# One core, a layer pair over 16 sequences: a new written order for every engine, and two waits on GpSimd

## The chip, the cores and the metric

The kernel runs on one core of a Trainium2 chip. The metric is the device time of one execution, in microseconds (us); lower is better. The core has five engines with instruction streams of their own: PE (TensorE, matmuls), DVE (VectorE), ACT (ScalarE), POOL (GpSimd) and SP (SyncE, which here only issues DMAs). They meet through semaphores.

## The reference, cut to what matters

The input is x of 16 sequences, 512 tokens, 128 channels. Two layers, each an attention part and a feed-forward part, each with a residual and a layer norm:

```python
x = layernorm(x + L0_attn(x))   # RWKV time mixing and channel mixing
x = layernorm(x + L0_ffn(x))    # soft binary tree: 255 gates, 256 leaves
x = layernorm(x + L1_attn(x))   # rms norm, 16 heads of 8 channels, RoPE, causal softmax
x = layernorm(x + L1_ffn(x))    # 16 experts, the 2 best by softmax, 2 shared ones
```

The time mixing has a key k, a value v and a receptance r of 512 channels, two scans over the tokens, a quotient, and a product with sigmoid(r). The tree multiplies gate probabilities down 8 levels. The experts take the two largest of 16 probabilities per token.

## The kernel before, in words

A sequence is a batch b of 512 tokens, kept as 128 partitions x 4 token tiles or as 128 channels x 512 tokens. All 16 batches go through one software pipeline. ORDER (from line 50) is a list for each engine, written out by hand. An entry `lag:step` means that in turn t the engine does this step for batch t − lag; run() (L276) walks the list turn by turn, 20 turns in all. So in one turn five different batches are in work: time and channel mixing at lags 0 to 2, the tree and RoPE at lag 2, the attention at lags 2 and 3, the experts at lags 3 and 4. An engine does its steps strictly in that order; each step first waits for what it needs (`until`, `reached`) and then raises a semaphore (`raised`). The line in the profile is that of the instruction, or of the helper that issues it (L488 is every plain copy of ACT, L905 every matmul, L638 every scalar_tensor_tensor).

The steps that matter here:

- `row0` to `row39` on PE compute the scores whose maxima `rowmax0` to `rowmax39` on DVE take (L725, L728), through two banks in turn. `max_parts` (L731) then splits the maxima into three bfloat16 parts in four dependent operations on DVE (L733, L638, L737, L739). `maxT` on PE (turn_maxima, L1068) transposes them, `maxT_out` on ACT copies them and `max_rows` on SP sends them by DMA to the queries. Only then `score0` to `score39` and `exp0` to `exp39` begin. I call the first the row stage, the second the score stage.
- The experts: `gb0` to `gb15` on PE spread a gate over all partitions in bank G. The even ones are multiplied with the input by DVE (`u0`, `u2`, ... L808). The odd ones are copied by ACT (`spread1`, ...), then multiplied on POOL (`u1`, `u3`, ... gated_input, L436). `expert0` to `expert15` on PE use them.
- Time mixing, four chunks c of 128 channels: `k`, `v`, `r` on PE; `clamp`, `kv`, `ksum`, `kvsum`, `wkv`, `inverse` on DVE (L651, L657, L662, L667, L638, L675); `k_exp`, `k_first`, `r_tanh` on ACT; `r_sig`, `wk`, `gated`, `rwkv` on POOL (L385, L381, L390, L395). `r` of chunk c waits for `clamp` c (L924).
- Channel mixing: `cmk` on PE, `cmk_tanh` on ACT, `silu` on DVE, `cmr_sig` and `cmr_sum` on POOL (L403, L408), `y0` on DVE (L694), which waits for cmr_sum.
- `tree0` to `tree7` on DVE (L638): two dependent operations per level, twice as many values at each.
- `largest0`, `others`, `largest1`, `gates` on DVE (L784 to L802): the two picks of the router, small operations on 128x64. `others` writes `left` (L638). After `others` the semaphore `pick` stands at 5 for the batch.
- `moments` n on DVE and `root` n on POOL (L344 to L355) prepare a layer norm; `norm` n on ACT applies it. `res` on POOL (L399) adds the residual; `x1_gain`, `x1_bias` on POOL (L372, L376).

Three forms of working on SBUF matter: an operation of DVE may read PSUM and one SBUF operand (rowmax, kv, u, clamp) or two SBUF operands (max_rest, left, tree, the scans); POOL reads SBUF alone.

## Time and profile before

| | |
|---|---|
| median of 3 runs | 1956.96 us (1956.66 to 1959.65) |
| the profiled execution | 1953.77 us, span 1951.9 us |
| busy in the span | PE 1677.3 us (86%), DVE 1554.8 (80%), ACT 1009.0 (52%), POOL 889.5 (46%) |
| mean granted TensorE clock | 0.962 of full speed |
| one turn in the middle of the run | 109.9 us |

The page of the profile gives the busy time of each engine, the chain of work that ended last, and groups of instructions. The timeline view gives start and duration in us, engine, line, operation, output <- inputs and a count; what stands in brackets at the end is how long the engine sat idle before it and what ended that. Several like instructions in a row are merged into one line, so ends of neighbouring rows may overlap a little. In the profile `prob`, `tree` and `x` are also names for buffers that hold other values at other times: u writes `prob`, and the thing called x in `thr<-thr,x` is x0.

### The profile page before, as it was taken

The page shows a single profiled execution, that of the slowest core. Times are in us where ns is not written, and L with a number is a line of the kernel's source. Part 1 is how long each engine was busy: PE and PEld are TensorE (multiplying, and loading weights), DVE is VectorE, ACT ScalarE, POOL GpSimd, SP SyncE. Part 2 cuts the span into 40 slices and gives each one's busy share as a digit, 9 for nine tenths or more (in the row PEclk, how much of TensorE's full clock was granted, in tenths as well). Part 3 has the DMA queues.
Part 4 walks back from the last instruction along what each step waited for, and adds up shares of the span by engine and source line. Part 5 has one row for each costly group of instructions (what it writes and reads, how often), then busy time and mean ns, then how long its engine had stood idle before and what let it go on. Part 6 is the DMA issues. An engine that isn't in the chain of part 4 may idle for free.

```text
span 1951.9 us, 34254 instructions
## 1 busy us (share of the span) xinstructions
PE 1677.3 (86%) x12161; PEld 1088.7 (56%) x12269; DVE 1554.8 (80%) x3386; ACT 1009.0 (52%) x1998; POOL 889.5 (46%) x1120
## 2 busy tenths in 40 slices
...
GB/s 98 0 6 54 2 53 5 45 16 18 45 3 60 2 55 7 38 24 14 49 2 60 2 55 8 33 29 10 53 2 61 2 55 1 31 26 22 35 7 6
DMA packets 66924, 53.39 MB, mean 27 GB/s; under 512 B 8322, under 2 KB 65474, under 8 KB 66754
## 3 DMA queue, kind: packets, MB, share of 16 engines
...
q10 hardware_dynamic: 3552, 1.65, 0.3%
...
## 4 chain that ended last, share of the span: by engine, by line
PE 49%; DVE 33%; POOL 6%; ACT 5%; issue 5%; SPq 1%; DMA 0%; ACTq 0%; DVEq 0%; POOLq 0%; another core or an unknown queue 0%
PE bank L905 47%; DVE rmax L728 10%; PE bank L901 3%; DVE prob L808 3%; DVE stats L629 3%; ACT prob L488 2%; DVE rmax L725 2%; DVE mixed L638 2%; POOL rstd L351 2%; ACT xd L494 1%; DVE mv L634 1%; DVE kvsum L667 1%; SPq L325 1%; DVE left L638 1%; POOL x L399 1%
## 5 line engine op out<-in xcount | busy, mean ns | idle before, releaser
L488 ACT ACTIVATE prob<-bank 128x512 f32<-128x512 f32 x640 | 357.4, 597 | 95.5 <-PE bank L905 88.4
L728 DVE TENSOR_REDUCE rmax<-bank 128x1 f32<-128x512 f32 (+2 forms) x768 | 353.7, 502 | 14.6 <-PE bank L905 13.1
L436 POOL TENSOR_TENSOR prob<-xdT,spread 128x512 f32<-128x512 f32 x128 | 162.2, 1267 | 354.6 <-ACT spread L488 354.6
L905 PE MATMUL bank<-kh,qh 72*128 72x512 bf16 (+3 forms) x1024 | 266.6, 308 | 45.2 <-DVE rmax L728 36.3
L905 PE MATMUL bank<-wexpT,prob 128*128 128x128 f32 x2048 | 278.1, 284 | 0.8 <-POOL prob L436 0.6
L905 PE MATMUL bank<-qh,kh 75*128 75x512 bf16 (+3 forms) x1024 | 256.5, 304 | 20.6 <-ACT prob L488 17.8
L905 PEld LDWEIGHTS bank<-wexpT,prob 128*128 128x128 f32 x2048 | 259.9, 198 | 19.0 <-issue 12.5
L488 ACT ACTIVATE spread<-bank 128x512 f32<-128x512 f32 x128 | 76.4, 597 | 338.2 <-PE bank L905 330.1
L905 PEld LDWEIGHTS bank<-qh,kh 75*128 75x128 bf16 x1024 | 100.1, 98 | 206.9 <-ACT prob L488 138.2
L675 DVE RECIPROCAL wkb<-wkb 128x512 f32<-128x512 f32 x64 | 211.5, 3325 | 0.0
L905 PE MATMUL bank<-maskb,identb 128*128 128x128 bf16 x1024 | 194.4, 223 | 0.0
L905 PE MATMUL bank<-maskTb,identb 128*128 128x128 bf16 x1024 | 193.3, 221 | 0.0
L905 PEld LDWEIGHTS bank<-kh,qh 72*128 72x128 bf16 x1024 | 101.6, 99 | 143.5 <-DVE rmax L728 93.2
L905 PE MATMUL bank<-prob,vaug 128*32 128x512 f32 (+3 forms) x2048 | 176.2, 445 | 3.0 <-ACT prob L488 2.9
L347 POOL TENSOR_TENSOR var<-mv,eps_ln 128x4 f32<-128x4 f32 x112 | 27.7, 247 | 230.8 <-DVE mv L634 230.2
L905 PEld LDWEIGHTS bank<-maskb,identb 128*128 128x128 bf16 x1024 | 102.4, 100 | 39.0 <-issue 23.5
L381 POOL TENSOR_TENSOR wkb<-wkb,ksum 128x512 f32<-128x512 f32 x64 | 93.6, 1463 | 64.7 <-DVE ksum L662 56.5
L905 PEld LDWEIGHTS bank<-maskTb,identb 128*128 128x128 bf16 x1024 | 101.3, 99 | 24.2 <-issue 22.6
L351 POOL TENSOR_TENSOR rstd<-var,exponent 128x4 f32<-128x4 f32 x112 | 113.8, 1016 | 1.2
L488 ACT ACTIVATE rth<-bank 128x512 f32<-128x512 f32 x128 | 75.4, 589 | 68.4 <-PE bank L905 60.8
L395 POOL TENSOR_TENSOR inner<-rth,wkb 128x512 f32<-128x512 f32 x64 | 82.4, 1287 | 56.9 <-DVE wkb L675 55.3
L808 DVE TENSOR_TENSOR prob<-xdT,bank 128x512 f32<-128x512 f32 x128 | 86.9, 679 | 26.0 <-PE bank L905 22.4
...
## 6 DMA issues: line engine op xcount, KB each, us to landing
...
```

The costliest lines, as they stand in the source:

```text
L351: raised(pool.tensor_tensor(rstd[:, n, :], var[:, n, :], exponent[:, :], ALU.pow), f"root{n}")
L381: raised(pool.tensor_tensor(wkb[:, c % 2, :], wkb[:, c % 2, :], ksum[:, c % 2, 0:T], ALU.add), "wk")
L395: raised(pool.tensor_tensor(inner[:, c, :], rth[:, c % 2, :], wkb[:, c % 2, :], ALU.mult), "rwkv")
L436: raised(pool.tensor_tensor(ug[:, e % 4, :], xdT[:, :], spread[e // 2 % 2][:, :], ALU.mult), "ug_side")
L488: raised(act.activation(dst, src, func, **kw), signal)
L629: last = dve.bn_stats(stats[:, n, j, :], t[:, j, :])
L638: return dve.scalar_tensor_tensor(out=out_, in0=in0, scalar=scalar, in1=in1, op0=op0, op1=op1)
L675: raised(dve.reciprocal(wkb[:, c % 2, :], wkb[:, c % 2, :]), "wk_inv")
L728: last = dve.tensor_reduce(rmax[:, j, h:h + 1], S[n % 2][:, col:col + (j + 1) * P], AX_X, ALU.max)
L808: raised(dve.tensor_tensor(ug[:, e % 4, :], xdT[:, :], G, ALU.mult), "ug")
L901: last = pe.transpose(bk[:, j * P:(j + 1) * P], t[:, j, :], ident[:, :])
L905: return pe.matmul(out_, w, x, start=start, stop=stop, **kw)
```

## The change

The order of each engine's list is written anew; the steps in it are the same. (The names busy_rows1 and busy_experts1 become busy_rows2 and busy_experts2, which do the same.) On POOL two waits are added: cmr_sum of batch b waits until `others` of batch b − 2 is done (both are in the same turn), and u15 of batch b waits until max_parts of batch b + 1 is done (again the same turn).

```diff
--- before.py
+++ after.py
@@ -49,44 +49,44 @@
 
 ORDER = dict(
     sp="""
-        2:heads0 2:heads1 4:store 0:load 2:max_rows
+        2:heads0 2:heads1 0:load 2:max_rows 4:store
     """,
     pool="""
-        4:u3 4:u5 4:u7 4:u9 4:u11 4:u13 1:r_sig0 1:wk0 1:gated0 4:u15 1:r_sig1 1:rwkv0 4:root7 1:wk1 1:gated1 0:root0 2:root_rms 1:r_sig2 1:gated2 1:rwkv1
-        1:wk2 2:root4 1:wk3 2:rope_sum0 1:r_sig3 2:rope_sum1 2:rest0 1:gated3 1:rwkv2 1:rwkv3 2:part_lo0 2:rest1 2:part_lo1 1:res 1:root2 0:x1_gain
-        0:x1_bias 0:root1 3:root6 1:cmr_sig 1:cmr_sum 3:gate_rest 3:gate_lo 1:root3 3:u1
+        0:root0 4:u3 1:r_sig0 4:u5 4:u7 4:u9 4:u11 4:u13 1:wk0 4:u15 1:gated0 1:r_sig1 1:rwkv0 4:root7 1:wk1 1:wk2 2:root_rms 1:r_sig2 1:gated1 1:rwkv1
+        1:gated2 1:wk3 2:rope_sum0 2:rope_sum1 2:rest0 1:r_sig3 1:gated3 1:rwkv2 2:part_lo0 1:rwkv3 2:rest1 2:part_lo1 1:root2 0:x1_gain 0:x1_bias 2:root4
+        1:res 0:root1 3:root6 1:cmr_sig 1:cmr_sum 3:gate_rest 3:gate_lo 1:root3 3:u1
     """,
     act="""
...
-        3:maxT_out 1:k_exp2 1:k_first1 1:r_tanh2 3:exp0 3:exp1 1:k_first2 3:exp2 3:exp3 3:exp4 3:exp5 3:exp6 3:exp7 2:leafT_out0 3:exp8 2:leafT_out1
...
-        3:pvT_out0 3:exp33 3:exp34 3:exp35 3:exp36 2:part_mid1 3:exp37 3:exp38 2:norm4 3:exp39 0:norm0 3:pvT_out1 2:values 1:norm2 3:attT_out
...
+        4:route_exp 2:cmk_tanh3 3:norm4 2:cmr_tanh 1:norm1 4:gate_hi 4:gate_mid 1:mix_before0 4:gT_out 1:mix_before1 1:mix_before2 4:spread1 3:vaug
...
+        4:spread15 1:k_first1 3:maxT_out 1:k_exp2 1:k_first2 3:exp0 3:exp1 1:r_tanh2 3:exp2 3:exp3 3:exp4 3:exp5 3:exp6 3:exp7 3:exp8 2:leafT_out0
...
+        3:exp32 3:pvT_out0 3:exp33 3:exp34 3:exp35 3:exp36 3:exp37 2:part_mid1 3:exp38 3:exp39 0:norm0 3:pvT_out1 1:norm2 3:attT_out 1:mix_before3
+        1:mix_before4 1:cmk_tanh0 2:values 3:norm6 1:cmk_tanh1 3:xdT_out 1:cmk_tanh2
     """,
     dve="""
-        3:rowmax18 1:clamp0 0:moments0 3:rowmax19 3:rowmax20 4:u4 1:ksum0 3:rowmax21 1:kv0 3:rowmax22 3:rowmax23 3:rowmax24 4:u6 1:kvsum0 2:tree0
-        3:rowmax25 3:rowmax26 2:tree1 3:rowmax27 3:rowmax28 4:u8 3:rowmax29 3:rowmax30 1:clamp1 2:tree2 3:rowmax31 4:u10 3:rowmax32 2:tree3 3:rowmax33
-        4:u12 3:rowmax34 3:rowmax35 1:wkv0 3:rowmax36 3:rowmax37 4:u14 3:rowmax38 3:rowmax39 3:max_parts 1:inverse0 1:clamp2 1:kv1 2:tree4 2:tree5
-        1:kvsum1 2:tree6 2:tree7 4:yd 4:moments7 1:wkv1 1:kv2 1:ksum1 1:kvsum2 1:clamp3 1:wkv2 2:yb 2:moments4 1:inverse1 1:kv3 1:kvsum3 1:ksum2 1:wkv3
-        2:rope_mul0 2:rope_mul1 1:ksum3 2:rope_mul2 2:rope_mul3 1:inverse2 1:inverse3 3:attend0 1:x2 1:moments2 3:attend1 0:moments1 3:yc 1:mix3
-        3:moments6 2:rowmax0 1:mix4 2:rowmax1 2:rowmax2 1:silu0 2:rowmax3 2:rowmax4 1:silu1 1:silu2 3:route_logits 2:rowmax5 3:route_probs 1:silu3
-        3:largest0 3:others 3:largest1 2:rowmax6 3:gates 2:rowmax7 1:y0 2:rowmax8 2:rowmax9 1:moments3 2:rowmax10 2:rowmax11 3:u0 2:rowmax12 0:mix0
-        2:rowmax13 2:rowmax14 0:mix1 2:rowmax15 2:rowmax16 3:u2 0:mix2 2:rowmax17
+        0:moments0 3:rowmax18 1:clamp0 3:rowmax19 3:rowmax20 1:kv0 4:u4 3:rowmax21 1:ksum0 3:rowmax22 3:rowmax23 1:kvsum0 2:tree0 3:rowmax24 3:rowmax25
+        4:u6 2:tree1 3:rowmax26 3:rowmax27 3:rowmax28 3:rowmax29 4:u8 3:rowmax30 1:clamp1 3:rowmax31 3:rowmax32 4:u10 2:tree2 3:rowmax33 1:wkv0 3:rowmax34
+        4:u12 3:rowmax35 2:tree3 3:rowmax36 3:rowmax37 4:u14 3:rowmax38 3:rowmax39 3:max_parts 1:inverse0 2:tree4 1:clamp2 1:kv1 2:tree5 2:tree6 2:tree7
+        1:ksum1 4:yd 4:moments7 1:kvsum1 1:wkv1 1:clamp3 1:kv2 1:ksum2 1:kvsum2 2:yb 2:moments4 1:inverse1 1:wkv2 1:kv3 1:kvsum3 1:ksum3 1:wkv3
+        2:rope_mul0 2:rope_mul1 2:rope_mul2 2:rope_mul3 1:inverse2 1:inverse3 1:x2 1:moments2 3:attend0 3:attend1 0:moments1 3:yc 1:mix3 3:moments6
+        2:rowmax0 2:rowmax1 1:mix4 2:rowmax2 2:rowmax3 1:silu0 1:silu1 2:rowmax4 1:silu2 3:route_logits 2:rowmax5 3:route_probs 1:silu3 3:largest0
+        2:rowmax6 3:others 2:rowmax7 3:largest1 2:rowmax8 3:gates 2:rowmax9 1:y0 2:rowmax10 2:rowmax11 2:rowmax12 1:moments3 3:u0 2:rowmax13 0:mix0
+        2:rowmax14 2:rowmax15 0:mix1 0:mix2 2:rowmax16 3:u2 2:rowmax17
     """,
     pe="""
...
-        4:expert14 4:expert15 1:r2 3:score0 3:score1 1:v2 3:score2 3:score3 1:k3 3:score4 3:score5 3:score6 2:leafT0 3:score7 3:score8 2:leafT1 3:weigh0
...
-        2:busy_rows0 3:attT 1:xn2T 3:attn_out 2:busy_rows1 2:row0 2:row1 1:cmk0 3:busy_experts1 2:row2 1:cmk1 2:row3 2:row4 3:xdT 1:cmk2 3:centroids
-        1:cmk3 2:row5 3:shared 1:cmr 2:row6 1:cmv0 2:row7 1:cmv1 1:cmv2 1:cmv3 2:row8 2:row9 3:busy_gates1 0:xnT 3:gT 2:row10 2:row11 3:gb0 2:row12
...
-        3:expert5 2:row29 2:row30 3:gb9 3:expert6 2:row31 3:gb10 2:row32 3:expert7 0:r1 2:row33 3:gb11 3:expert8 3:gb12 2:row34 3:expert9 2:row35 0:v1
-        2:row36 3:gb13 2:row37 3:expert10 3:gb14 2:row38 2:row39 3:expert11 3:gb15 0:k2 2:maxT 3:expert12 3:expert13
+        4:expert15 1:r2 3:score0 3:score1 1:v2 3:score2 3:score3 2:leafT0 3:score4 3:score5 1:k3 3:score6 3:score7 2:leafT1 3:score8 3:weigh0 3:score9
...
+        2:busy_rows0 3:attT 1:xn2T 3:attn_out 2:busy_rows2 2:row0 2:row1 1:cmk0 3:busy_experts2 2:row2 2:row3 1:cmk1 2:row4 3:xdT 1:cmk2 2:row5
+        3:centroids 1:cmk3 2:row6 3:shared 1:cmr 1:cmv0 2:row7 2:row8 1:cmv1 2:row9 1:cmv2 1:cmv3 2:row10 3:busy_gates1 2:row11 0:xnT 2:row12 3:gT 2:row13
...
+        2:row29 3:expert6 2:row30 2:row31 3:gb9 3:expert7 2:row32 3:gb10 3:expert8 2:row33 3:gb11 2:row34 0:r1 2:row35 3:gb12 3:expert9 3:gb13 2:row36
+        2:row37 3:expert10 3:gb14 2:row38 2:row39 3:expert11 3:gb15 0:k2 0:v1 2:maxT 3:expert12 3:expert13 3:expert14
     """,
 )
 
@@ -405,6 +405,7 @@
             def channel_sum(b):
                 until(pool, b, "cmr_sig")
                 until(pool, b, "res")
+                until(pool, b - 2, "pick", 5)
                 raised(pool.tensor_tensor(thr[:, :, :], thr[:, :, :], x0[b % 2][:, :, :], ALU.add), "cmr_sum")
 
             def rope_sum(b, t):
@@ -433,6 +434,8 @@
                 until(pool, b, "spread_out", e // 2 + 1)
                 if e >= 4:
                     until(pool, b, "expert_ps", e - 3)
+                if e == NE - 1 and b + 1 < B:
+                    until(pool, b + 1, "max_part")
                 raised(pool.tensor_tensor(ug[:, e % 4, :], xdT[:, :], spread[e // 2 % 2][:, :], ALU.mult), "ug_side")
```

In PE's list, not all of which is shown, expert14 moves from the head of the turn to its end, which is the same place in the stream; v1 moves from behind row35 to behind k2, ahead of maxT; gb13 from behind row36 to ahead of it; gT from behind row9 to behind row12; leafT0 from behind score6 to behind score3. In ACT's list norm4 moves from behind exp38 to the head of the next turn, and `values` from ahead of norm2 to behind cmk_tanh0.

## Rows read from the trace of the kernel before

**Rows 1.** The page, part 4: the chain that ended last, shares by engine.
```profile
PE 49%; DVE 33%; POOL 6%; ACT 5%; issue 5%; SPq 1%; DMA 0%; ACTq 0%; DVEq 0%; POOLq 0%; another core or an unknown queue 0%
```

**Rows 2.** Windows (us): busy of PE, PEld, DVE, ACT, POOL; granted clock; DMA.
```profile
980.00:991.00 11.00, 10.89 (x80) 8.34 (x81) 10.12 (x23) 2.99 (x6) 5.21 (x5) 1.00 0.01 1
994.50:1038.00 43.50, 42.34 (x342) 25.09 (x342) 36.75 (x54) 33.87 (x66) 28.63 (x33) 1.00 0.07 17
884.60:994.50 109.90, 100.77 (x758) 65.82 (x765) 96.65 (x210) 62.19 (x123) 54.71 (x68) 1.00 0.10 28
```

**Rows 3.** Timeline of DVE: the splitting of the maxima and what follows.
```profile
990.99 0.46 DVE L733 TENSOR_SCALAR max_cols<-rmax 128x64 bf16<-128x64 f32 x1
991.49 1.22 DVE L638 SCALAR_TENSOR_TENSOR max_rest<-rmax,max_cols 128x64 f32<-128x64 f32 x1
992.74 1.15 DVE L737 CAST max_cols<-max_rest 128x64 bf16<-128x64 f32 x1
993.92 0.57 DVE L739 TENSOR_TENSOR max_cols<-max_rest,max_cols 128x64 bf16<-128x64 f32 x1
994.42 3.34 DVE L675 RECIPROCAL wkb<-wkb 128x512 f32<-128x512 f32 x1
997.68 0.62 DVE L651 TENSOR_SCALAR kk<-bank 128x512 f32<-128x512 f32 x1
```

**Rows 4.** Timeline of POOL beside rows 3.
```profile
991.36 1.26 POOL L390 TENSOR_TENSOR rth<-rth,kvb 128x512 f32<-128x512 f32 x1
...
997.91 1.27 POOL L395 TENSOR_TENSOR inner<-rth,wkb 128x512 f32<-128x512 f32 x1 [3.48 <-DVE wkb L675]
```

**Rows 5.** Tile view, DVE: duration ns min/median/max, first and last start, forms.
```profile
L638 DVE SCALAR_TENSOR_TENSOR max_rest<-rmax,max_cols x16: 224/1216/1218, 219.8 to 1855.3; 128x64 f32<-128x64 f32 x16
L737 DVE CAST max_cols<-max_rest x16: 194/1154/1156, 220.1 to 1855.6; 128x64 bf16<-128x64 f32 x16
L739 DVE TENSOR_TENSOR max_cols<-max_rest,max_cols x16: 225/570/1218, 220.3 to 1855.8; 128x64 bf16<-128x64 f32 x16
...
L638 DVE SCALAR_TENSOR_TENSOR left<-hot,pe_ x16: 224/1332/1335, 286.1 to 1914.3; 128x64 f32<-128x64 f32 x16
```

**Rows 6.** Timeline of PE around the transpose of the maxima.
```profile
985.90 1.07 PE L905 MATMUL bank<-mixed,wv 128*128 128x512 f32 x2
...
994.55 0.40 PE L905 MATMUL bank<-identb,max_cols 128*128 128x128 bf16 x4 [2.88 <-DVE max_cols L739]
994.78 3.79 PE L905 MATMUL bank<-wexpT,prob 128*128 128x128 f32 x32
998.41 1.07 PE L905 MATMUL bank<-mixed,wr 128*128 128x512 f32 x2
```

**Rows 7.** Timeline of DVE: the pick that stands beside cmr_sum.
```profile
948.78 1.33 DVE L638 SCALAR_TENSOR_TENSOR left<-hot,pe_ 128x64 f32<-128x64 f32 x1
```

**Rows 8.** Timeline of POOL: cmr_sum.
```profile
948.76 1.27 POOL L408 TENSOR_TENSOR thr<-thr,x 128x512 f32<-128x512 f32 x1
```

**Rows 9.** Timeline of DVE: three early levels of the tree.
```profile
975.87 0.96 DVE L638 SCALAR_TENSOR_TENSOR tree<-tree 128x8 f32<-128x8 f32 x2
...
980.39 1.09 DVE L638 SCALAR_TENSOR_TENSOR tree<-tree 128x16 f32<-128x16 f32 x2
...
983.26 0.41 DVE L638 SCALAR_TENSOR_TENSOR tree<-tree 128x32 f32<-128x32 f32 x2
```

**Rows 10.** Timeline of POOL: root1 and root6 after the residual.
```profile
935.90 0.20 POOL L347 TENSOR_TENSOR var<-mv,eps_ln 128x4 f32<-128x4 f32 x1 [1.40 <-DVE mv L634]
...
938.32 0.20 POOL L347 TENSOR_TENSOR var<-mv,eps_ln 128x4 f32<-128x4 f32 x1 [0.82 <-DVE mv L634]
...
939.71 0.20 POOL L355 TENSOR_TENSOR shift<-minus,rstd 128x4 f32<-128x4 f32 x1
```

**Rows 11.** Timeline of DVE: the third silu.
```profile
943.95 0.69 DVE L638 SCALAR_TENSOR_TENSOR inner<-rth,bank 128x512 f32<-128x512 f32 x1 [0.76 <-ACT rth L488]
```

**Rows 12.** Waits in total: us, times, longest.
```profile
DVE prob L808 <- PE bank L905: 22.4, 36, 3.4
```

More of the change, by code:

```diff
@@ L62 @@
-        3:maxT_out 1:k_exp2 1:k_first1 1:r_tanh2 3:exp0 3:exp1 1:k_first2 3:exp2 3:exp3 3:exp4 3:exp5 3:exp6 3:exp7 2:leafT_out0 3:exp8 2:leafT_out1
-        3:exp9 3:exp10 4:norm7 3:exp11 3:exp12 1:k_exp3 3:exp13 3:exp14 3:exp15 3:exp16 3:exp17 3:exp18 2:norm_rms 3:exp19 3:exp20 2:xcT_out 3:exp21
-        3:exp22 1:r_tanh3 3:exp23 1:k_first3 3:exp24 3:exp25 3:exp26 3:exp27 3:exp28 2:part_hi0 3:exp29 3:exp30 2:part_hi1 2:part_mid0 3:exp31 3:exp32
-        3:pvT_out0 3:exp33 3:exp34 3:exp35 3:exp36 2:part_mid1 3:exp37 3:exp38 2:norm4 3:exp39 0:norm0 3:pvT_out1 2:values 1:norm2 3:attT_out
@@ L66 @@
-        1:mix_before3 1:mix_before4 1:cmk_tanh0 3:norm6 1:cmk_tanh1 3:xdT_out 1:cmk_tanh2
+        4:route_exp 2:cmk_tanh3 3:norm4 2:cmr_tanh 1:norm1 4:gate_hi 4:gate_mid 1:mix_before0 4:gT_out 1:mix_before1 1:mix_before2 4:spread1 3:vaug
+        2:norm3 4:spread3 2:xbT_out 1:k_exp0 1:r_tanh0 2:gate0 4:spread5 2:gate1 4:spread7 4:spread9 4:spread11 1:k_first0 1:k_exp1 1:r_tanh1 4:spread13
+        4:spread15 1:k_first1 3:maxT_out 1:k_exp2 1:k_first2 3:exp0 3:exp1 1:r_tanh2 3:exp2 3:exp3 3:exp4 3:exp5 3:exp6 3:exp7 3:exp8 2:leafT_out0
@@ new lines @@
+        2:leafT_out1 3:exp9 3:exp10 4:norm7 3:exp11 3:exp12 1:k_exp3 3:exp13 3:exp14 3:exp15 3:exp16 3:exp17 3:exp18 2:norm_rms 3:exp19 3:exp20 2:xcT_out
+        3:exp21 3:exp22 1:k_first3 3:exp23 3:exp24 3:exp25 1:r_tanh3 3:exp26 3:exp27 2:part_hi0 3:exp28 3:exp29 2:part_hi1 3:exp30 2:part_mid0 3:exp31
+        3:exp32 3:pvT_out0 3:exp33 3:exp34 3:exp35 3:exp36 3:exp37 2:part_mid1 3:exp38 3:exp39 0:norm0 3:pvT_out1 1:norm2 3:attT_out 1:mix_before3
+        1:mix_before4 1:cmk_tanh0 2:values 3:norm6 1:cmk_tanh1 3:xdT_out 1:cmk_tanh2
@@ L84 @@
-        2:busy_rows0 3:attT 1:xn2T 3:attn_out 2:busy_rows1 2:row0 2:row1 1:cmk0 3:busy_experts1 2:row2 1:cmk1 2:row3 2:row4 3:xdT 1:cmk2 3:centroids
-        1:cmk3 2:row5 3:shared 1:cmr 2:row6 1:cmv0 2:row7 1:cmv1 1:cmv2 1:cmv3 2:row8 2:row9 3:busy_gates1 0:xnT 3:gT 2:row10 2:row11 3:gb0 2:row12
-        3:biases 2:row13 3:gb1 2:row14 3:expert0 2:row15 2:row16 3:gb2 1:xbT 3:expert1 2:row17 2:row18 3:gb3 0:k0 0:v0 2:row19 2:row20 3:gb4 0:r0
-        3:expert2 2:row21 3:gb5 2:row22 1:gates0 2:row23 1:gates1 2:row24 3:gb6 0:k1 3:expert3 2:row25 3:gb7 2:row26 3:expert4 2:row27 3:gb8 2:row28
```

12 lines of the change are left out of this document (6 added, 6 removed).

## The prediction

> **What bounds the kernel now.** I read the chain that ended last first: it shares itself between PE (49%) and DVE (33%), and POOL has 6% [rows 1]. So POOL's own time is not what is paid for; the question is what it does to the other two. Next, the windows, cut where one turn of the pipeline ends and the next begins, at the transpose of the maxima: a turn takes 109.9 us, with PE busy for 100.8 and DVE for 96.7 of it [rows 2]. The bound changes inside the turn. In the score stage (43.5 us) PE is busy for 42.3 and DVE for 36.8, so PE sets it; at the end of the row stage (980 to 991) PE is busy for 10.9 of 11.0 and DVE for 10.1, so both are nearly full, and earlier in the rows DVE is.
>
> Then the timelines of DVE and POOL beside each other, where what passes between them shows. The four operations of max_parts work on 128x64 values. They take 0.46, 1.22, 1.15 and 0.57 us, from 990.99 to 994.49 [rows 3]; the shortest of the same instructions took 0.22, 0.19 and 0.23, and started about 0.25 apart [rows 5]. Beside them POOL ran gated0, from 991.36 to 992.62 [rows 4]: max_rest, issued at 991.49, ended at 992.71, just behind it, and the others likewise behind POOL's next instructions. So a DVE operation that reads and writes SBUF does not run more slowly beside GpSimd, it waits until GpSimd's instruction is over. `left` does the same: 1.33 us [rows 7] beside cmr_sum, 948.76 to 950.03 [rows 8], against 0.22 at its shortest [rows 5].
>
> **The change part by part**, per turn. A minus is a gain.
>
> **1. The split maxima.** Four operations 0.25 apart are 1.0 us in place of 3.5: DVE gives back 2.45 [rows 3, 5]. The new wait lies ahead of u15 on POOL. Behind it there queue gated0, r_sig1, rwkv0 and root7, and PE's expert15 waits for u15. The maxima's end releases u15 and it takes about 1.27 (as rows 8, same form). Expert15 is the last quarter of a 3.8 us block behind the transpose [rows 6], 0.23 + 2.8 us after it, so u15 arrives 1.7 us early: nothing is paid. wk0, which the reciprocal needs, now stands ahead of u15.
>
> PE stood idle for 2.88 us ahead of the transpose [rows 6]. The change also takes v1 out of the last rows and puts it there. It records 1.07 us, of which 0.16 overlaps what follows (994.78 + 3.79 against 998.41, rows 6), so 0.91 net. The gap of 2.88 less 2.45 is covered by v1, and the transpose comes 2.88 − 0.91 = 1.97 earlier after the last row.
>
> But the next thing PE meets is r2, which waits for clamp2. Before, clamp2 stood straight behind the reciprocal and ended at 998.30, and r2 began at 998.41: already tied [rows 3, 6]. Now tree4 stands between them, and rwkv0 on POOL starts 0.15 us after the reciprocal's end (994.42 + 3.34 against 997.91; rows 3, 4) and holds for 1.27. Tree4's first operation gets through; the second waits until 1.42 after the reciprocal. Clamp2 then starts at about 1.65 and ends at 1.0 + 3.3 + 1.65 + 0.6 = 6.55 after the last row maximum, where it was 7.3. **Gain −0.8.** Without that collision tree4 costs about 0.5 (two operations of 0.22 to 0.25, rows 5), clamp2 ends at 5.4, and the gain is −1.9. Both ends are kept; I take −0.8, since rwkv0's row shows it ready 0.15 us behind the reciprocal, and nothing in the change moves it.
>
> The Trainium skill (GPSIMD Engine Reference, Key points) says GpSimd "shares its SBUF interfaces with VectorE", with contention from instructions in a two-port mode or with two SBUF inputs. Read as sharing, tree4's second operation would merely double, to about 0.5, clamp2 would be 0.25 late and not 1.15, and the gain of this part would be some −1.65 and not −0.8. The rows above speak for exclusion, and it is that which the sum uses.
>
> **2. The last rows.** tree1 took 0.96 and tree2 1.09 us where tree3, with more values, took 0.41 [rows 9]; 1.2 us is waiting. In the new order they stand straight behind u6 and u10, and POOL's matching u7 and u11 come only after PE and ACT have turned them over, so they are clear. DVE is full around tree1, which gives its 0.55; near tree2 PE is full, and there v1's departure (0.91) lets PE take the remaining 0.65. **Gain −1.2**, between −0.5 (PE takes none of the second) and −1.5.
>
> **3. The first picks.** cmr_sum waits for `left`, so `left` falls from 1.33 to 0.22: −1.1 [rows 5, 7]. Behind cmr_sum only gate_rest is queued on POOL, and y0 on DVE waits for it, which stands seven steps later. But cmr_sum now begins with `left`'s end and lasts 1.27; after rowmax7 (two reductions, about 0.7) the second pick's operations of two SBUF operands meet its last 0.3 to 0.4. **Gain −0.8**, between −0.3 and −1.1. Gates are formed two row maxima later; the expert chain has the less room (a rival below).
>
> **4. Between the score and the row stages.** Before, POOL idled for 1.40 us up to 935.90, when moments1 was ready; so it was free at 934.50 [rows 10]. Root1 ended well ahead of root6, which began at 938.32 after 0.82 idle. Now root4 (as root6, 938.32 to 939.91, so 1.6) and the residual (1.27, as rows 8) stand ahead of root1: 934.5 + 1.6 + 1.3 = 937.4, root1 to 939.0, and root6 starts 0.7 late. Behind root6 come norm6, the transpose xdT, and on PE behind that cmk2, whose tanh the third silu waits for; DVE already stood 0.76 idle there [rows 11]. Silu1 and silu2 also stand ahead of rowmax4 and have less to hide behind. **Loss +0.7**, between 0 and +1.0. Moving attend0 behind moments2 fills DVE's idle time there; `values` behind norm2 frees ACT: nothing either way.
>
> **5. Moved at no cost.** root0 now leads POOL's turn, so u3 comes about 2 us later; expert3 stands behind row23 in PE's order, several microseconds on, and u5 is unaffected. SP: the store moves from ahead of the load to behind the maxima's DMA. It issues behind a 0.8 us issue, its rows are only needed by norm7 of the next turn over 10 us later, and the heads' 36 DMAs of SP come after it. norm4 leaves the score stage for ACT's idle time at the head of the turn; yc reads its output only at the turn's end. In the score stage DVE may lose some waits, but PE is full there [rows 2], so this only widens a margin.
>
> **Sum.** −0.8 − 1.2 − 0.8 + 0.7 = −2.1 us per turn. `left` has a mean of 1193 ns over 16, (1193 − 224) / 1108 = 14 contended ones (rows 5 give the ends); so 14 turns, −29 us. The profiled execution took 1953.8 us (span 1951.9), 3.2 below the median of the runs; I subtract from the median: 1956.96 − 29.4 = 1927.6, say 1927.
>
> **Rivals.**
> *Everything is kept* (0.22). No collision at tree4 and the xd chain hidden: −1.9 − 1.2 − 1.1 = −4.2, times 14 is −59: 1898. For: the idle 2.88 us of PE and the 1.40 us of POOL, into which most of root4 fits. Against: rows 3, 4 and 11.
> *PE takes it* (0.12). PE is busy for 92% of the turn; if each row waits for PE, parts 2 and 3 shrink to −0.5 and −0.3, and the turn gains 0.3 to 0.9: 1944 to 1953. For: 10.9 of 11.0 us. Against: parts of the rows where PE is 90% busy.
> *The waits don't move anything* (0.05): the instructions waited for are not those which collide, the split maxima stay at 3.5, and ±0.2%: 1953 to 1961. Against: the wait names precisely them.
> *The expert chain turns into the bound, slower* (0.11). The gates' transpose stands behind row12 in place of row9, yet expert11 is still behind the last row, so fifteen handovers PE, DVE, PE, ACT share the fewer rows. DVE's eight u operations wait little so far: 22.4 us over the kernel, 36 waits, but single ones of 3.4 [rows 12]. If each waits 0.5 us more, that is +4.0 per turn against −2.1: +1.9, times 14 is +27, 1984. It decides from 0.26 us for each of the eight. Against: the two-row delay is small beside some 30 us.
>
> **How the numbers follow.** My own case (0.50) reaches from 1917 to 1941 with the bounds of its parts. The range takes in the full gain and nearly all of PE's case: 1893 to 1953. A measurement of this kernel tells about 0.2% (4 us) from no change. Faster: 0.50 + 0.22 + 0.12 = 0.84; same 0.05; slower 0.11.
>
> **What would show it.** The three later max_parts operations near 0.22 us and `left` near 0.22; PE's 2.88 us ahead of the transpose gone, and in its place a wait of r2 for clamp2 of about 1.1 us, with tree4 at over 1.2; root6 starting later after moments6; the turn at 107.8. Wrong, if tree4 is short and r2 doesn't wait (1898), if the row stage keeps its length, or if DVE's u operations wait for PE in the tens of us more.

## The result, and the profile after

| | before | after |
|---|---|---|
| median | 1957.07 us of 4 runs (1956.66 to 1959.65) | 1892.22 us of 4 runs (1889.09 to 1893.33) |
| ratio to before | 1 | 0.966 [0.965, 0.968] |
| the profiled execution | 1953.77, span 1951.9 | 1891.78, span 1890.0 |
| busy: PE, DVE, ACT, POOL | 1677.3, 1554.8, 1009.0, 889.5 | 1668.7, 1503.1, 1020.8, 931.3 |

Faster by 3.4%: 65 us where 29 were forecast, and just below the range. (All line numbers stand 1 to 3 higher in the kernel after.) The page of after, its head and the chain that ended last:

```profile
PE 1668.7 (88%) x12162; PEld 1083.8 (57%) x12269; DVE 1503.1 (80%) x3386; ACT 1020.8 (54%) x1998; POOL 931.3 (49%) x1120
...
PE 49%; DVE 26%; POOL 9%; ACT 6%; issue 4%; SPq 2%; DMA 2%; ACTq 0%; DVEq 0%; POOLq 0%; another core or an unknown queue 0%
```

DVE does the same operations in 51.7 us less, and its share of the chain falls from 33% [rows 1] to 26%, while POOL is busy for 42 us more. Some of what used to be time of DVE standing behind POOL is now time of POOL standing behind DVE: an instruction that is waiting counts as busy, and POOL's longest of the form 128x512 in a steady turn takes 2.20 us in after, 1.86 in before.

The timeline of DVE in after, around the splitting of the maxima (start, us, engine, line, operation):

```profile
965.27 0.20 DVE L736 TENSOR_SCALAR max_cols<-rmax 128x64 bf16<-128x64 f32 x1
965.50 0.23 DVE L641 SCALAR_TENSOR_TENSOR max_rest<-rmax,max_cols 128x64 f32<-128x64 f32 x1
965.75 0.20 DVE L740 CAST max_cols<-max_rest 128x64 bf16<-128x64 f32 x1
965.99 0.23 DVE L742 TENSOR_TENSOR max_cols<-max_rest,max_cols 128x64 bf16<-128x64 f32 x1
966.13 3.35 DVE L678 RECIPROCAL wkb<-wkb 128x512 f32<-128x512 f32 x1
969.39 0.42 DVE L641 SCALAR_TENSOR_TENSOR tree<-tree 128x64 f32<-128x64 f32 x2
969.77 0.69 DVE L654 TENSOR_SCALAR kk<-bank 128x512 f32<-128x512 f32 x1
```

The same stretch on POOL:

```profile
966.38 1.27 POOL L439 TENSOR_TENSOR prob<-xdT,spread 128x512 f32<-128x512 f32 x1 [1.65 <-DVE max_cols L742]
967.61 1.27 POOL L390 TENSOR_TENSOR rth<-rth,kvb 128x512 f32<-128x512 f32 x1
968.85 0.61 POOL L385 TENSOR_SCALAR rth<-rth 128x512 f32<-128x512 f32 x1
969.62 1.33 POOL L395 TENSOR_TENSOR inner<-rth,wkb 128x512 f32<-128x512 f32 x1 [0.16 <-DVE wkb L678]
```

and on PE:

```profile
965.78 1.02 PE L908 MATMUL bank<-mixed,wv 128*128 128x512 f32 x2
966.64 0.39 PE L908 MATMUL bank<-identb,max_cols 128*128 128x128 bf16 x4
966.86 3.79 PE L908 MATMUL bank<-wexpT,prob 128*128 128x128 f32 x32
970.51 1.13 PE L908 MATMUL bank<-mixed,wr 128*128 128x512 f32 x2
```

The four operations take 0.95 us, from 965.27 to 966.22, where they took 3.5 [rows 3]: u15 waits 1.65 us for them and comes behind. PE's gap of 2.88 us ahead of the transpose [rows 6] is gone. But two rows contradict the forecast. tree4's two operations took 0.42 together, not held up by rwkv0, and r2 starts at once, with no wait for clamp2.

The DVE timeline of after at the picks, with the wait of cmr_sum on POOL in a fence of its own:

```profile
925.36 0.75 DVE L731 TENSOR_REDUCE rmax<-bank 128x1 f32<-128x384 f32 x2
926.02 0.23 DVE L641 SCALAR_TENSOR_TENSOR left<-hot,pe_ 128x64 f32<-128x64 f32 x1
926.17 0.68 DVE L731 TENSOR_REDUCE rmax<-bank 128x1 f32<-128x512 f32 x1
926.77 0.20 DVE L787 TENSOR_REDUCE m<-left 128x4 f32<-128x64 f32 x1
927.00 0.77 DVE L789 TENSOR_TENSOR eq<-left,m 128x64 f32<-128x64 f32 x1
```

```profile
926.42 1.27 POOL L409 TENSOR_TENSOR thr<-thr,x 128x512 f32<-128x512 f32 x1 [0.24 <-DVE left L641]
```

`left` is short now, and `eq`, the next operation with two SBUF inputs, stands behind cmr_sum instead, as forecast: 0.77 where it was 0.22.

**Where the time went.** I cut each steady turn of both kernels at five landmarks and took the median of ten turns, in us:

| stretch | before | after |
|---|---|---|
| A: transpose of the maxima to the start of x2 (score stage) | 43.62 | 44.01 |
| B: to the copy of the route logits (handover) | 16.31 | 16.75 |
| C: to y0 (picks) | 8.42 | 8.37 |
| D: to the first operation of max_parts (rows) | 38.01 | 35.14 |
| E: to the transpose (split) | 3.56 | 1.37 |
| one turn, median (mean) | 109.93 (110.55) | 105.64 (105.74) |

In after, two steps of row maxima (1.27 us together) stand in C which stood in D before. Like for like, C gained 1.32 and D 1.60. Between the first transpose and the last there are 15 turns: 1636.50 before, 1569.30 after, so −67.2. The way to the first transpose became 5.1 us longer (220.57 to 225.72), the rest stayed within 0.2. Together −61.9, the difference of the two spans.

**The turns that had been longer.** The median turn of before is 109.93, the mean 110.55. The difference is what four of the ten turns have in stretch A, 45.2 in place of 43.6. The timeline of PE in before, in such a turn:

```profile
773.13 0.40 PE L905 MATMUL bank<-identb,max_cols 128*128 128x128 bf16 x4 [2.88 <-DVE max_cols L739]
773.36 5.42 PE L905 MATMUL bank<-wexpT,prob 128*128 128x128 f32 x32
```

and windows of before within this block and within the same block of the next turn (busy of PE, PEld, DVE, ACT, POOL; granted clock; DMA share; GB/s):

```profile
773.40:776.40 3.00, 3.00 (x21) 3.00 (x19) 3.00 (x2) 0.59 (x1) 0.00 (x0) 0.64 0.05 14
...
884.80:888.40 3.60, 3.60 (x36) 3.60 (x33) 3.60 (x3) 0.59 (x1) 0.42 (x1) 1.00 0.05 14
```

Straight behind the 2.88 us in which PE did nothing, the granted clock was at its lower level for most of the next 3 us (0.64 is a mean of 0.5 and 1, that is of 1.2 and 2.4 GHz), and the 32 matmuls took 5.42 us where they take 3.79 at the upper level [rows 6]. This happened in 4 of the 13 turns that have the gap of 2.88, and once more behind the 2.17 us ahead of the last transpose but one (5.26): 5 of 15 such blocks. In after all 15 blocks take 3.79.

### The profile page after: what moved, and what is told of

Same layout as the page of the kernel before. It is cut to its first block, busy times and chain, and to the rows that moved or that the text cites. A ratio compares the mean times of both kernels' runs of the same rounds, so it can differ in the third digit from the quotient of the medians.

```text
span 1890.0 us, 34255 instructions
## 1 busy us (share of the span) xinstructions
PE 1668.7 (88%) x12162; PEld 1083.8 (57%) x12269; DVE 1503.1 (80%) x3386; ACT 1020.8 (54%) x1998; POOL 931.3 (49%) x1120
## 3 DMA queue, kind: packets, MB, share of 16 engines
q10 hardware_dynamic: 3552, 1.65, 0.3%
## 4 chain that ended last, share of the span: by engine, by line
PE 49%; DVE 26%; POOL 9%; ACT 6%; issue 4%; SPq 2%; DMA 2%; ACTq 0%; DVEq 0%; POOLq 0%; another core or an unknown queue 0%
PE bank L908 47%; DVE rmax L731 6%; DVE wkb L678 3%; POOL rstd L351 3%; PE bank L904 3%; ACT prob L491 2%; DVE tree L641 2%; DVE stats L632 2%; DVE rmax L728 1%; ACT xd L497 1%; POOL inner L395 1%; DVE prob L811 1%; DMA qh<-part 1%; SPq L325 1%; DVE inner L641 1%
## 5 line engine op out<-in xcount | busy, mean ns | idle before, releaser
L439 POOL TENSOR_TENSOR prob<-xdT,spread 128x512 f32<-128x512 f32 x128 | 168.0, 1313 | 234.0 <-ACT spread L491 206.6
L908 PE MATMUL bank<-wexpT,prob 128*128 128x128 f32 x2048 | 267.0, 278 | 2.3 <-POOL prob L439 0.7
L908 PEld LDWEIGHTS bank<-wexpT,prob 128*128 128x128 f32 x2048 | 250.0, 192 | 8.9 <-POOL prob L439 0.9
L347 POOL TENSOR_TENSOR var<-mv,eps_ln 128x4 f32<-128x4 f32 x112 | 33.1, 296 | 339.3 <-DVE mv L637 339.3
L381 POOL TENSOR_TENSOR wkb<-wkb,ksum 128x512 f32<-128x512 f32 x64 | 111.3, 1747 | 42.4 <-DVE ksum L665 21.4
L351 POOL TENSOR_TENSOR rstd<-var,exponent 128x4 f32<-128x4 f32 x112 | 120.8, 1079 | 1.3
L811 DVE TENSOR_TENSOR prob<-xdT,bank 128x512 f32<-128x512 f32 x128 | 87.0, 679 | 22.4 <-PE bank L908 17.2
L390 POOL TENSOR_TENSOR rth<-rth,kvb 128x512 f32<-128x512 f32 x64 | 96.0, 1500 | 14.5 <-DVE kvb L641 13.1
```

What stands on the lines that cost most here:

```text
L351: raised(pool.tensor_tensor(rstd[:, n, :], var[:, n, :], exponent[:, :], ALU.pow), f"root{n}")
L381: raised(pool.tensor_tensor(wkb[:, c % 2, :], wkb[:, c % 2, :], ksum[:, c % 2, 0:T], ALU.add), "wk")
L390: raised(pool.tensor_tensor(rth[:, c % 2, :], rth[:, c % 2, :], kvb[:, c % 2, :], ALU.mult), "gated")
L439: raised(pool.tensor_tensor(ug[:, e % 4, :], xdT[:, :], spread[e // 2 % 2][:, :], ALU.mult), "ug_side")
L811: raised(dve.tensor_tensor(ug[:, e % 4, :], xdT[:, :], G, ALU.mult), "ug")
L908: return pe.matmul(out_, w, x, start=start, stop=stop, **kw)
```

## The experiments

Each edit of an order is shown by the steps that change places. A time "per turn" is the median turn's.

**1. The two waits taken away or put alone.** *a_no_u15_wait* is after without the first of these, *b_no_pick_wait* after without the second, *c_waits_only* is before with both.

```diff
-                if e == NE - 1 and b + 1 < B:
-                    until(pool, b + 1, "max_part")
...
-                until(pool, b - 2, "pick", 5)
```

> The kernel after the change without the wait of u15 for the split maxima. In the profile of after, u15 was ready at 964.73 and waited 1.65 us; the four operations of max_parts ran from 965.27 to 966.22. Theory (the two engines exclude each other, the wait keeps POOL out): u15 runs from 964.73 to 966.0 and gated0 from there to 967.2, so max_rest waits until 966.0 (+0.5) and the cast until 967.2 (+1.2); max_parts takes about 2.7 us in place of 0.95, PE, which had 0.5 us to spare ahead of the transpose, waits 1.2 us, and the turn goes from 105.65 to about 106.9. Over 14 turns +17, and a few TensorE clock drops behind the idle gap may come back: 1905 to 1918 us. Rival (the new order alone does it, the wait is idle): max_parts stays at 0.95 and the time within 4 us of 1892.

> The kernel after without the wait of cmr_sum for the first picks. In the profile of after the wait cost POOL 0.24 us only, and the operation eq of the second pick took 0.77 us in place of 0.22 behind cmr_sum. Theory (exclusion): cmr_sum starts 0.24 us earlier, at about 926.18, while rowmax6 is running and ahead of `left` (926.02): either it lies just behind `left`, and nothing changes but 0.24 us less for eq, or it gets in first and `left` takes 1.2 to 1.4 us in place of 0.23, with eq back at 0.22, so +0.5 to +0.7 per turn. 1888 to 1902 us, more likely the upper half. Rival: the wait is what the gain of the picks hangs on (1.1 us per turn), 1907.

> The kernel before with the two waits alone, in its old order. Theory (exclusion, parts add): gated0 still stands ahead of u15 and still runs beside max_rest (1.2 us), but the cast and the last operation fall to 0.20 and 0.22, so max_parts goes from 3.5 to about 2.0 us, and PE's idle time ahead of the transpose from 2.88 to about 1.4. `left` falls from 1.33 to 0.22. Per turn 1.5 + 1.1 = 2.6 us less, turn 107.3, and the TensorE clock drops behind the gap (8 us in all) are fewer: 1957 - 36 - 5 = 1916, range 1908 to 1930. Rival (the waits do nothing without the new order): 1953 to 1961.

| | median | ratio to before | turn | A | C | E |
|---|---|---|---|---|---|---|
| a_no_u15_wait | 1909.36 | 0.977 [0.975, 0.978] | 106.64 | 44.39 | 8.37 | 1.99 |
| b_no_pick_wait | 1892.72 | 0.968 [0.967, 0.969] | 105.49 | 44.01 | 8.21 | 1.37 |
| c_waits_only | 1929.45 | 0.987 [0.985, 0.988] | 108.53 | 43.62 | 8.33 | 2.25 |

Without its wait, u15 lands on the last of the four operations. DVE and POOL of *a_no_u15_wait*, timelines:

```profile
972.51 1.22 DVE L740 TENSOR_TENSOR max_cols<-max_rest,max_cols 128x64 bf16<-128x64 f32 x1
```

```profile
972.38 1.26 POOL L437 TENSOR_TENSOR prob<-xdT,spread 128x512 f32<-128x512 f32 x1 [1.13 <-ACT spread L489]
```

That costs 1.00 per turn, 17 us in all: 0.62 in E, and 0.38 in A, where r2 now waits for clamp2. So the new order with the picks' wait gains 2.3%, and the wait of u15 the last 1%. The wait of cmr_sum gives nothing: without it a turn is even 0.15 shorter, and the two medians cannot be told apart. In *c_waits_only* `left` is short, but `eq` two operations behind it takes over the whole collision; DVE timeline of *c_waits_only*:

```profile
939.50 0.23 DVE L641 SCALAR_TENSOR_TENSOR left<-hot,pe_ 128x64 f32<-128x64 f32 x1
939.76 0.22 DVE L787 TENSOR_REDUCE m<-left 128x4 f32<-128x64 f32 x1
940.01 1.23 DVE L789 TENSOR_TENSOR eq<-left,m 128x64 f32<-128x64 f32 x1
```

A wait that frees one operation hands the collision to the next of the same kind. What gains is that the row maxima, which read the matmuls' banks, now stand in between.

**2. Parts of the order undone.** *d_v1_back* puts v1 behind row35 again, *e_tree4_back* puts tree4 behind kv1, *f_res_first* takes the residual ahead of root2 on POOL, as it was.

```diff
-2:row35 3:gb12      ... 0:k2 0:v1 2:maxT
+2:row35 0:v1 3:gb12 ... 0:k2 2:maxT
...
-1:inverse0 2:tree4 1:clamp2 1:kv1
+1:inverse0 1:clamp2 1:kv1 2:tree4
...
-1:root2 0:x1_gain 0:x1_bias 2:root4 1:res 0:root1
+1:res 1:root2 0:x1_gain 0:x1_bias 2:root4 0:root1
```

> The kernel after with v1 back behind row35 on PE. Theory: the end of the row stage has PE full, so v1's 0.9 us is paid there, and ahead of the transpose PE idles for 0.3 to 0.5 us: the turn goes from 105.65 to about 106.1 to 106.5, 1892 + 6 to 12 = 1898 to 1904. Rival (DVE sets the last rows, PE has room there): the turn stays within 0.2 us, 1889 to 1895.

> The kernel after with tree4 back behind clamp2 and kv1. My prediction held that rwkv0 on POOL gets in between the two operations of tree4, which stand behind the reciprocal; the profile of after shows both tree operations over in 0.42 us and rwkv0 running behind them (969.62, 1.33 us). Theory (POOL's instruction comes 0.16 us behind the reciprocal and finds the lock held; DVE's next one is through in time): with clamp2 and kv1 there instead, which read PSUM, rwkv0 gets in at once and tree4 waits for its end, about 0.4 us lost before tree5, as in the kernel before (1.38 us for four operations); leafT0, which already waits 0.23 us for the tree, waits 0.4 more: turn +0.4, 1892 + 5 = 1897. Rival (my prediction's reading): moving tree4 away from rwkv0 saves time, at least 0.2 us per turn, 1889 or less.

> The kernel after with the residual on POOL back ahead of root2. Theory: POOL idles there (3.79 us ahead of root2), so the residual is free, and root1 and root6 come 1.2 us earlier than in after, as far as moments6 lets them: root6 starts 0.45 us earlier after x2, norm6 and xdT too, the turn 105.65 - 0.45 = 105.2. Over 15 turns -6: 1886. Rival (DVE sets the early rows, xdT has slack): the turn stays at 105.6, 1892.

| | median | ratio to before | turn | A | B | D | E |
|---|---|---|---|---|---|---|---|
| d_v1_back | 1903.31 | 0.973 [0.972, 0.975] | 106.55 | 44.38 | 16.75 | 36.06 | 1.00 |
| e_tree4_back | 1896.36 | 0.970 [0.969, 0.972] | 105.94 | 44.32 | 16.74 | 35.13 | 1.37 |
| f_res_first | 1888.21 | 0.966 [0.964, 0.967] | 105.18 | 44.00 | 16.31 | 35.13 | 1.37 |

Behind row35, v1 adds 0.92 to D and takes 0.37 from E, but A grows by the same 0.37. PE timeline of *d_v1_back*:

```profile
971.79 0.40 PE L908 MATMUL bank<-identb,max_cols 128*128 128x128 bf16 x4 [0.32 <-DVE max_cols L742]
972.03 3.79 PE L908 MATMUL bank<-wexpT,prob 128*128 128x128 f32 x32
976.04 1.12 PE L908 MATMUL bank<-mixed,wr 128*128 128x512 f32 x2 [0.22 <-DVE kk L654]
```

Here is the wait of r2 for clamp2 that I had forecast. An earlier transpose only waits later: in after, the row of clamp2 ends at 970.46 and r2 begins at 970.51, so v1 fills exactly time that PE could not have used. Its move is worth 0.91 per turn. tree4's place is worth 0.30 in A, and that not by way of r2, which has no wait in either: leafT0, further on, waits 0.57 us for the tree in place of 0.23. The residual's new place costs 0.44 in B: root6 and the third silu come that much later. Undoing it gives a turn 0.46 shorter than after's, though the intervals of the medians overlap.

**3. Is the clock drop a matter of the gap?** *g_busy_before* is before with the matmuls that only keep PE busy (they write a bank that nothing reads) ahead of the transpose; the work is otherwise unchanged. *h_v1_only* is before with v1 there.

```diff
-0:k2 2:maxT
+0:k2 2:busy_maxima0 2:busy_maxima1 2:busy_maxima2 2:maxT
```

> The kernel before with six idle matmuls (three of its own busy steps, whose results nobody reads) ahead of the transpose of the maxima, into PE's gap of 2.88 us. They wait for u15, at 993.8 in the turn shown. In the kernel before, five of the 16 transposes are followed by a stretch of 3.4 us at half the granted TensorE clock, and the block of experts 12 to 15 takes 5.42 us there in place of 3.79. Theory (the drops come from the gap, not from elsewhere): with the gap partly filled the drops are gone or fewer, the block is 3.79 us in all turns: 1957 - 8 = 1949, with up to +0.5 us per turn (+7) where the last busy matmul ends behind 994.5. So 1947 to 1957. Rival (the drops are spread by chance): still four to six long blocks, 1957 or above.

> The kernel before with v1 alone moved from the last rows to behind k2. Theory: the gap ahead of the transpose falls from 2.88 to about 2.0 us; DVE, full in the last rows with its waits for POOL, gives back little: turn 109.9 - 0.3 to 0.6, and the TensorE clock drops behind the gap are gone or fewer (-4 to -8): 1940 to 1950. Rival (PE sets the last rows): the turn falls by the whole 0.9 us, 1957 - 13 - 8 = 1936.

| | median | ratio to before | turn (mean) | A | D | E |
|---|---|---|---|---|---|---|
| g_busy_before | 1947.86 | 0.997 [0.995, 0.998] | 109.93 (109.94) | 43.62 | 38.01 | 3.56 |
| h_v1_only | 1941.35 | 0.993 [0.992, 0.995] | 109.26 (109.26) | 43.62 | 37.62 | 3.28 |

*g_busy_before* leaves every stretch as it was and only removes the long turns: the mean falls from 110.55 to 109.94 and the time by 0.35% [0.24, 0.47]. PE timeline of *g_busy_before*:

```profile
991.94 0.40 PE L905 MATMUL bank<-identb,max_cols 128*128 128x128 bf16 x4 [1.45 <-DVE max_cols L739]
992.18 3.79 PE L905 MATMUL bank<-wexpT,prob 128*128 128x128 f32 x32
```

With 1.45 us idle in place of 2.88 no turn shows the slower block. In *h_v1_only* the gap is 1.72 in the steady turns, and none of them has it; it comes once, behind the 2.17 us ahead of the last transpose but one. Its view of the transpose's tile (what PE's idle time before it ended on: us, times):

```profile
  DVE max_cols L739: 26.9, 15
```

In *h_v1_only* the turn shrinks by 0.67: 0.39 in D and 0.28 in E.

**4. The picks and the trees alone, in the old order.**

```diff
-3:largest0 3:others 3:largest1 2:rowmax6 3:gates 2:rowmax7 1:y0
+3:largest0 2:rowmax6 2:rowmax7 3:others 3:largest1 3:gates 1:y0
```

```diff
-2:tree1 3:rowmax27 3:rowmax28 4:u8 3:rowmax29 3:rowmax30 1:clamp1 2:tree2 3:rowmax31 4:u10
+3:rowmax27 3:rowmax28 4:u8 2:tree1 3:rowmax29 3:rowmax30 1:clamp1 3:rowmax31 4:u10 2:tree2
```

> The kernel before with no new wait, and only DVE's order around the picks changed: rowmax6 and rowmax7 stand between largest0 and others, so `left` and the second pick come 1.27 us later, behind cmr_sum's end. The run with the two waits alone showed that the wait of cmr_sum moves the loss from `left` (0.23) to eq of the second pick (1.23) and gains 0.09 us from the router's logits to y0. Theory (only DVE work of another kind put in between takes the loss away): `left` and eq both at 0.22, the stretch from the logits to y0 falls from 8.42 to 7.3 us, turn 109.93 - 1.1 = 108.8; the clock drops ahead of the experts' block stay: 1954 - 15 = 1939, range 1934 to 1946. Rival (PE holds the early rows, so time won on DVE is lost again before y0 or in the next rows): turn not under 109.5, 1948 or more.

> The kernel before with only tree1 and tree2 moved on DVE: straight behind u8 and u10, ahead of the time at which POOL's next u starts. Both then take about 0.4 us in place of 0.96 and 1.09, 1.2 us less. Theory (PE is full in the last rows, so part is lost): y0 to the splitting of the maxima falls from 38.01 to 37.2 to 37.6, turn -0.4 to -0.8: 1954 - 6 to 11 = 1943 to 1948. Rival (DVE alone sets the rows): -1.2 per turn, 1937.

> The kernel before with the trees moved and v1 moved as well. v1 alone gave 0.39 us in the rows and 0.28 ahead of the transpose, 0.67 per turn, and took most clock drops away. Theory (PE and DVE hold each other in the last rows, so each alone is worth less than its size): together the rows give 1.2 + 0.3 or more, 38.01 to 36.5 or below, and the turn 109.93 - 1.9 = 108.0, more than v1's 0.67 and the trees' own value added: 1954 - 27 - 6 = 1921, range 1917 to 1928. Rival (they add): 109.93 - 0.67 - the value of the trees alone (0.4 to 0.8), 108.5 to 108.9, 1928 to 1936.

| | median | ratio to before | turn | A (longest) | C | D | E |
|---|---|---|---|---|---|---|---|
| i_picks_only | 1946.22 | 0.994 [0.993, 0.996] | 109.62 | 44.27 (46.43) | 7.32 | 38.03 | 3.56 |
| j_trees_only | 1953.67 | 0.998 [0.996, 0.999] | 110.74 | 44.98 (45.20) | 8.43 | 37.45 | 3.56 |
| k_trees_and_v1 | 1932.57 | 0.987 [0.986, 0.989] | 108.73 | 43.62 (43.62) | 8.43 | 37.06 | 3.28 |

*i_picks_only* gains its whole −1.10 in C, with no new wait at all: two row maxima behind the first pick are enough for cmr_sum to pass. *j_trees_only* gains 0.56 in D. Yet little of it shows in their times (16.5 and 8.4 us would be 15 turns of it; 0.6% and 0.2% came): of the 13 turns with the gap of 2.88, 4 have the slower block in before, 7 in *i_picks_only* and 10 in *j_trees_only*, in one profiled execution each. Both medians missed what was expected. PE timeline of *i_picks_only*, one of the longer ones:

```profile
771.64 5.37 PE L905 MATMUL bank<-wexpT,prob 128*128 128x128 f32 x32
```

With v1 in the gap (*k_trees_and_v1*) all of that is gone from the steady turns, and D is −0.95 = −0.56 − 0.39, exactly the sum of trees and v1. My theory here had been that the two help each other; the rival, that they add, was right.

**5. A better version.** *l_after_plus* is after with the residual first (as f), without the wait of cmr_sum (as b) and with one more row maximum ahead of the second pick. *p_best* is the same, with leafT0 behind score5.

```diff
-3:largest1 2:rowmax8 3:gates
+2:rowmax8 3:largest1 3:gates
...
-3:score3 2:leafT0 3:score4 3:score5 1:k3
+3:score3 3:score4 3:score5 2:leafT0 1:k3
```

> A version meant to beat both: the kernel after, with the residual ahead of root2 (gave 0.44 us per turn alone), without the wait of cmr_sum for the picks (0.16), and with rowmax8 on DVE ahead of largest1, so that eq comes behind cmr_sum's end (0.60 to 0.22). Theory (all three add, DVE sets the early rows): turn 105.65 - 0.44 - 0.16 - 0.38 = 104.67, 1888 to 1892 - 14 = 1876 to 1880. Rival (PE sets these rows once DVE is relieved): only the residual's part, 1886 to 1890.

> The version of the residual first, no pick wait and rowmax8 ahead of largest1, with leafT0 moved on PE from behind score3 to behind score5, so that it does not stand waiting for the tree (0.23 us in after). Theory: the score stage falls from 44.03 to 43.7 to 43.8 us, turn 104.96 - 0.25 = 104.7, 1887 - 3.5 = 1883. Rival (the stage's 0.4 us is bound by exp and rwkv3 instead): no change, 1887.

*l_after_plus*: 1887.22, ratio 0.964 [0.962, 0.965], turn 104.96, of which B 16.32 and C 8.09; the best of this study, 5 us below after. The expectation was missed: `eq` is at 0.23 now, 0.54 less, but C falls by only 0.28, since y0 now begins 0.05 behind the row maximum ahead of it, where it began at once in after, and the row maxima interleave differently; the rest is not resolved. *p_best*: 1888.81, 0.966 [0.964, 0.967], A 44.25 against 44.03: no gain. Removing leafT0's wait of 0.23 us for the tree did not shorten A. Windows over A show why it could not have been the 0.39 by which A grew: PE is idle for 1.11 us there in both kernels, and busy for 42.51 us in before and 42.90 in after, with the same matmuls. Why they take longer in the new order is open.

**6. Two terms measured on their own.** *m_tree2_collides* is after with tree2 where POOL is working. *n_max_parts_clear* is before with nothing but the wait of u15 and gated0 behind u15.

```diff
-4:u10 2:tree2 3:rowmax33 1:wkv0 3:rowmax34
+4:u10 3:rowmax33 1:wkv0 3:rowmax34 2:tree2
```

```diff
-1:wk0 1:gated0 4:u15 1:r_sig1
+1:wk0 4:u15 1:gated0 1:r_sig1
```

> The kernel after with tree2 alone moved on DVE, from behind u10 to behind rowmax34, where POOL's u11 is running (959.24 to 960.70 in the profile of after). tree2 takes about 1.0 to 1.1 us in place of 0.38. Theory (in the new order PE has room in the last rows, v1 being gone, so DVE time counts in full): y0 to the splitting of the maxima from 35.14 to about 35.8, turn 105.64 + 0.7 = 106.3, 1892 + 10 = 1902; together with picks, tree1 and v1 this closes the sum of the rows. Rival (PE withholds it there too, as in the old order, where clearing both trees gave 0.56 of 1.2 us): turn within 0.2 us, 1892 to 1895, and the half microsecond comes from elsewhere.

> The kernel before in its old order, with the wait of u15 for the split maxima and gated0 on POOL moved behind u15; nothing else. Theory (exclusion is the whole of it): the four operations fall to 0.20, 0.22, 0.20 and 0.22, the stretch from the first of them to the transpose from 3.56 to 1.0 us, PE's idle time from 2.88 to 0.4, and the clock drops are gone: turn 107.4, 1957 - 36 - 6 = 1915, range 1910 to 1922. Rival 1 (another limit comes in behind, r2's wait for clamp2 among them): the turn falls by less than 2.2 us, 1925 or more. Rival 2 (my first bounds: the reciprocal and rwkv0 take it up): 1930 or more.

*m_tree2_collides*: 1901.91, 0.973 [0.971, 0.974]. DVE timeline of *m_tree2_collides*:

```profile
965.51 0.87 DVE L641 SCALAR_TENSOR_TENSOR tree<-tree 128x16 f32<-128x16 f32 x2
```

0.87 where after has 0.38, and D grows from 35.14 to 35.63: the 0.49 us of DVE come out one for one in the turn (106.14). In the new order DVE bounds the rows; PE took none of it.

*n_max_parts_clear*: 1915.9, 0.980 [0.978, 0.981], as expected. E is 1.26, every other stretch is exactly before's, and no turn has the slower block. **Two edits on POOL, u15's wait and its place ahead of gated0, give 40 of the 65 us.** Per turn: −2.30 in E, and −0.62 as the long turns of before are gone. In the profiled executions the 15 turns together are 37.9 us shorter (the last ones gain less than the middle ones), the way to the first transpose is 2.7 longer and the rest 1.1 shorter: 36.4 of the 61.9 us between the spans of before and after.

## Why the prediction was wrong

The mechanism was right, the size too small by half: −2.1 per turn was forecast, −4.3 came (median), −4.8 with the long turns of before. The case that I gave 0.22, everything is kept (1898), was the nearest. By the steps of the prediction:

**Part 1, the split maxima (−0.8 forecast, −2.2 measured in E, and 2.3 alone): the step that failed.** DVE's 2.45 were right (3.5 to 0.95). What failed is the sentence that tree4's first operation gets through and the second waits for rwkv0. rwkv0 came where it was forecast, 0.16 us behind the reciprocal, at 969.62. But the second operation of tree4 had begun before it, as a narrow window on DVE of after shows:

```profile
969.59 0.23 DVE L641 SCALAR_TENSOR_TENSOR tree<-tree 128x64 f32<-128x64 f32 x1
```

It is first by 0.03 us in all 13 turns that have this sequence, and takes its usual 0.23; rwkv0 takes 1.33 in place of 1.27. So clamp2 ends 5.2 us after the first of the four operations (965.27 to 970.46), where 6.55 was forecast, 5.4 without the collision, and 7.3 was measured before. I had counted from the reciprocal's end. Rows 3 show DVE's next instruction beginning 0.08 ahead of that end (994.42 + 3.34 against 997.68), and the second of two short ones follows 0.20 to 0.25 later, so 0.12 to 0.17 behind the end; rwkv0 stood at 0.15. The rows left open which of the two would be first, and the outcome hung on 0.03 us. The range kept the case's other end (−1.9), and "What would show it" names this very sign; the choice between them was the error, and 1.4 of the 2.2 us per turn that the sum missed lie in this part, 1.1 of them in this choice.

The passage on sharing or exclusion stands. POOL's instruction is waited out whole in *a_no_u15_wait* (0.23 to 1.22 us). The other direction is seen at the scans of after, DVE and then POOL:

```profile
980.00 1.22 DVE L665 TENSOR_TENSOR_SCAN ksum<-decay,kk 128x512 f32<-128x512 f32 x1
981.13 2.05 DVE L670 TENSOR_TENSOR_SCAN kvsum<-decay,kvb 128x512 f32<-128x512 f32 x1
```

```profile
980.00 4.27 POOL L381 TENSOR_TENSOR wkb<-wkb,ksum 128x512 f32<-128x512 f32 x2
```

The engines take turns: two POOL instructions of 1.27 take 4.27 together, and the second scan takes 2.05 where the first took 1.22. So the rule of the Trainium skill (GPSIMD Engine Reference, Key points) that the two engines share interfaces shows here as exclusion, from either side.

v1's price was right: 0.91 forecast, 0.92 in D (*d_v1_back*). That u15 is early enough for expert15 was right too, POOL's 1.65 us of waiting cost PE nothing.

**The clock drops: a term that the sum lacked.** It multiplied a typical turn, and my turn was one of the short ones. 5 of 15 blocks of before were slow, 1.6 us each (5.42 − 3.79; one 1.5), 8 us in all; *g_busy_before* gives back 0.35% [0.24, 0.47], some 7 us, with the drops alone. The row stood in the trace: the turns of before do not all have the same length.

**Part 2, the last rows (−1.2 forecast, −1.6 in D).** The trees give 0.56 (*j_trees_only*) where 1.2 us of waiting had been seen, and v1 0.39. About 0.65 more came. Counted by what undoing costs in the new order, v1 is worth 0.92 (*d_v1_back*) and tree2 0.49 (*m_tree2_collides*), and only 0.2 is left for tree1 and the rest. I had 0.55 for tree1 and let v1's departure free the 0.65 of tree2. In the old order it did not: *k_trees_and_v1* has no more than trees and v1 each give alone. In the new one tree2's time counts in full.

**Part 3, the first picks (−0.8 forecast, −1.3 in C).** The size was 0.5 too small, and the cause wrong. I put it on the wait; *b_no_pick_wait* and *c_waits_only* show 0.1 or less for that, *i_picks_only* shows −1.10 for the two row maxima in between. The collision of `eq` came as forecast (0.77).

**Part 4 (+0.7 forecast, +0.44 in B), confirmed** by *f_res_first*, which gives back the same 0.44. What I had not foreseen is +0.39 in A, which is PE's own busy time and not a wait (experiment 5).

**Part 5** named moved work at no cost. In the steady turns nothing contradicts it; the 5.1 us that the way to the first transpose grew were not forecast and not isolated (*n_max_parts_clear* shows 2.7, *c_waits_only* 1.8, *h_v1_only* 1.5; with v1 back, after's falls by 2.3). From 180 us to the first transpose the granted clock is 0.83 in before, 0.78 in after and in *n_max_parts_clear*, and 0.84 in *d_v1_back*; whether that is the cause or follows from it no run separates.

**The sum took 14 turns**, from the collisions of `left`. The gains run over the 15 turns between the transposes: a small error, 2 us. The bounds of my own case (1917 to 1941) are narrower than those of its parts added up, −3.4 to −0.6 per turn, which over 14 turns is 1909 to 1949.

Of the rivals, "PE takes it" fell with the result, for which it had 0.3 to 0.9 per turn, and *m_tree2_collides* shows a stretch where PE takes nothing; "the waits don't move anything" fell with *a_no_u15_wait*, though it holds for one of the two waits; in the slower expert chain DVE's u operations were to wait for longer, but in after they wait 17.2 us for PE, less than the 22.4 of before [rows 12].
